# One attention kernel: the key-pair maxima of its first stage, regrouped so that left and right terms have PSUM banks of their own

## What is computed

```
q = layernorm(x) @ W_q + b_q          # 512 x 512: 16 heads of 32
k, v = split(ctx @ W_kv + b_kv)       # 8192 x 512 each
q, k = apply_rope(q, ...), apply_rope(k, ...)
attn = softmax(q @ k.T / sqrt(32))    # per head, 512 x 8192
x = x + (attn @ v) @ W_o + b_o
```

## Time and profile before

| | us |
|---|---|
| median of 3 runs (1836.43 to 1851.83) | 1842.03 |
| profiled execution, its time | 1842.78 |
| profiled execution, span of the profile | 1841.5 |
| PE busy, share of the span | 1653.6 (90%) |
| DVE busy | 1200.4 (65%) |
| ACT busy | 1120.4 (61%) |
| POOL busy | 689.7 (37%) |

### The profile page before, as it was taken

The page is one execution under the profiler, slowest core; times in us unless marked ns, Lnnn a source line. Parts: engine busy times, 40 slices in busy tenths (PEclk is TensorE's granted clock), DMA queues, the critical chain, the costliest instruction groups (busy, mean ns, idle before and its releaser), DMA issues.

```text
span 1841.5 us, 23809 instructions
## 1 busy us (share of the span) xinstructions
PE 1653.6 (90%) x8556; PEld 993.2 (54%) x8556; DVE 1200.4 (65%) x2691; ACT 1120.4 (61%) x1640; POOL 689.7 (37%) x323
## 2 busy tenths in 40 slices
PE   5669899998999965999999999999985998999998
PEld 4535555555555532333333333333574986888886
DVE  5447766777676765999898898898752553222222
ACT  3347666666666754977888888888731654333332
POOL 3166665666657742996000000000050004444442
PEclk7879999999999975999999999999997999999999
DMA  4644455445554437444444444455239003444431
GB/s 151 186 127 127 152 191 160 126 127 162 183 158 126 136 109 182 117 99 108 116 116 115 115 115 117 113 123 119 88 99 251 23 1 107 130 125 127 128 124 57
DMA packets 94949, 231.80 MB, mean 126 GB/s; under 512 B 11324, under 2 KB 11580, under 8 KB 89968
## 3 DMA queue, kind: packets, MB, share of 16 engines
q1 hardware_dynamic: 93792, 227.40, 44.5%
q10 hardware_dynamic: 1040, 2.88, 0.7%
HBM read 150.45 MB, written 59.84 MB: 114 GB/s over the span
## 4 chain that ended last, share of the span: by engine, by line
PE 57%; POOL 14%; DMA 7%; DVE 6%; issue 5%; ACT 5%; SPq 4%; POOLq 0%; ACTq 0%; DVEq 0%
PE PS L621 14%; PE PS L650 12%; PE PS L113 8%; PE PS L114 7%; PE PS L115 7%; DMA cs<-kr 5%; SPq L67 4%; POOL kr L385 4%; POOL kr L382 4%; POOL cs L383 4%; PE PS L418 3%; PE PS L903 2%; DVE rel L429 1%; ACT rel L426 1%; PE PS L660 1%
## 5 line engine op out<-in xcount | busy, mean ns | idle before, releaser
L627 ACT ACTIVATE P<-PS 128x1024 f32<-128x1024 f32 x512 | 494.5, 1024 | 92.5 <-PE PS L621 66.5
L639 DVE TENSOR_TENSOR acc<-acc,P 128x2048 f32<-128x2048 f32 x216 | 507.9, 2416 | 42.3 <-ACT P L627 42.1
L429 DVE CUSTOM_DVE_ANT_0 rel<-PS,rel 128x256 f32<-128x256 f32 x1024 | 373.1, 420 | 182.5 <-ACT rel L426 182.3
L426 ACT ACTIVATE rel<-PS 128x512 f32<-128x512 f32 x512 | 277.9, 596 | 130.0 <-PE PS L418 129.9
L650 PE MATMUL PS<-P,qe 128*32 128x512 f32 x2048 | 273.2, 606 | 0.0
L418 PE MATMUL PS<-khd,qh 32*128 32x512 f32 x1024 | 141.1, 534 | 101.1 <-DVE mpart L429 83.4
L108 POOL TENSOR_TENSOR w3l<-qk,w3h 128x2048 fp32r<-128x2048 f32 x2 | 9.1, 4559 | 490.7 <-ACT w3h L105 490.7
L108 POOL TENSOR_TENSOR El<-We,Eh 128x1536 fp32r<-128x1536 f32 x36 | 126.0, 3501 | 166.3 <-ACT Eh L105 166.2
L418 PEld LDWEIGHTS PS<-khd,qh 32*128 32x128 f32 x1024 | 59.7, 197 | 207.8 <-DVE mpart L429 193.7
L382 POOL TENSOR_TENSOR kr<-kr,cs 128x512 f32<-128x512 f32 x64 | 83.9, 1312 | 209.3 <-DMA cs<-kr 185.1
L1050 DVE TENSOR_TENSOR hf<-sg,PS 128x512 f32<-128x512 f32 x36 | 24.8, 688 | 193.2 <-PE PS L115 190.0
(11 more groups left out here) (208 smaller groups left out, 2876.5 us busy)
## 6 DMA issues: line engine op xcount, KB each, us to landing
khd<-kscr SPq DMA_DIRECT2D x129, 256.0 KB, 4.1
We<-in_w_e SPq DMA_DIRECT2D x36, 768.0 KB, 5.9
y<-in_y SPq DMA_DIRECT2D x16, 1024.0 KB, 7.2
cs<-kr SPq DMA_DIRECT2D x128, 128.0 KB, 6.4
vscr<-cs SPq DMA_DIRECT2D x16, 1024.0 KB, 4.8
kscr<-khd SPq DMA_DIRECT2D x16, 1024.0 KB, 6.8
kscr<-kl SPq DMA_DIRECT2D x16, 1024.0 KB, 7.0
qe<-vscr SPq DMA_DIRECT2D x64, 256.0 KB, 4.7
```

The source lines that it names most:

```text
L426: m = AC.sig(nc.scalar.activation(rel[b][:, :, :], PS[:, 2 * b:2 * b + 2, 256:512], ACT.Relu))
L429: maxfree[b] = DV.sig(nc.vector.tensor_tensor_reduce(out=rel[b][:, j, :], in0=PS[:, 2 * b + j, 0:256], in1=rel[b][:, j, :], scale=1.0, sca ...
L627: expm[s, pr] = spfree[b] = AC.sig(nc.scalar.activation(P[s % 4][:, 2 * pr:2 * pr + 2, :], PS[:, 2 * b:2 * b + 2, :], ACT.Exp, scale=SCALE))
L639: accm[s] = DV.sig(nc.vector.tensor_tensor(a[:, :, :], a[:, :, :], P[s % 4][:, :, :], ALU.add))
```

## The change

`maxima(c, i)` is gone. In its place a step treats two query blocks at once (`qp`, 8 steps for a chunk), in two halves. The three bank pairs are named r0, r1, r2.

1. `maxima_1`: for two query blocks, heads 0 and 1 are multiplied with the key columns themselves into r0, heads 2 and 3 with the difference columns into r1: 8 matmuls of 256 columns. ACT then takes relu of all of r1 (1024 elements).
2. `maxima_2`: heads 2 and 3 with the key columns into r1, heads 0 and 1 with the difference columns into r2: 8 matmuls. It waits for the relu that has just read r1. ACT takes relu of r2 (1024 elements). DVE does its four instructions on r1, then four on r0.

Then the roles turn by one pair (`cycle[0] += 1`). The number of DVE instructions (1024) and of columns streamed is the same; relu instructions are half as many and twice as long; matmuls and weight loads of the maxima are twice as many and half as long.

`mm3` now calls `tick` after each matmul, so a unit has 12 slots, and `at(u, m, fn)` names unit and slot. Places: `y_high` k in unit k of a chunk, slot 4 (before: all four in units 2 and 3); `y_low` unit 3, slot 4; `rope` as before at the end of unit 3; `key_high(c, g)` one unit apart, units 8+g (counted from the start of chunk c), slot 8; `key_low` at the end of unit 11; `maxima_1` and `maxima_2` at slots 2 and 7 of units 9 to 16.

```diff
-        maxfree = [None] * 3
-        pairs = [0]
+        maxfree, cycle, half = [None] * 3, [0], {}
...
+        def score_pairs(c, g, qp, which, left, right):
+            for t in range(2):
+                qt = 2 * qp + t
+                for hd in range(4):
+                    rows = slice(32 * hd, 32 * hd + 32)
+                    keys = slice(256, 512) if hd // 2 == which else slice(512, 768)
+                    o = PS[:, 2 * (left if hd // 2 == which else right) + hd % 2, t * 256:(t + 1) * 256]
+                    ins = nc.tensor.matmul(o, qh[rows, g, qt * 128:(qt + 1) * 128], khd[c % 2][rows, g, keys],
+                                           start=True, stop=True)
+            return PE.sig(ins)
...
+        def maxima_1(c, i):
+            g, qp = i // 2, i % 2
+            r = [(cycle[0] + j) % 3 for j in range(3)]
+            PE.wait(t_qsplit, khm[c, g], khd_m[c, g], maxfree[r[0]], maxfree[r[1]])
+            m = score_pairs(c, g, qp, 0, r[0], r[1])
+            half[c, i] = r, relu(0, r[1], m)
+        def maxima_2(c, i):
+            g, qp = i // 2, i % 2
+            r, t_r = half.pop((c, i))
+            cycle[0] += 1
+            PE.wait(maxfree[r[2]], t_r)
+            max_last[c] = m = score_pairs(c, g, qp, 1, r[1], r[2])
+            maxfree[r[2]] = t_l = relu(1, r[2], m)
+            maxfree[r[1]] = larger(c, g, qp, 1, 0, r[1], m, t_r)
+            maxfree[r[0]] = larger(c, g, qp, 0, 1, r[0], t_l)
...
-                    at_slot(32 * c + 9 + k, y_high, c + 1, k)
-                at_slot(32 * c + 12, y_low, c + 1)
-            at_slot(32 * c + 15, rope, c)
+                    at(8 * c + k, 4, y_high, c + 1, k)
+                at(8 * c + 3, 4, y_low, c + 1)
+            at(8 * c + 3, 11, rope, c)
             for g in range(4):
-                at_slot(32 * c + 38 + g, key_high, c, g)
-            at_slot(32 * c + 41, key_low, c)
-            for i in range(16):
-                at_slot(32 * c + 41 + 2 * i, maxima, c, i)
+                at(8 * c + 8 + g, 8, key_high, c, g)
+            at(8 * c + 11, 11, key_low, c)
+            for i in range(8):
+                at(8 * c + 9 + i, 2, maxima_1, c, i)
+                at(8 * c + 9 + i, 7, maxima_2, c, i)
```

More of the change, by code:

```diff
@@ L112, in mm3 @@
             for k in range(nk):
[L113 to L117, removed]
+                for i, (a_, b_) in enumerate(((lh, rh), (lh, rl), (ll, rh))):
+                    ins = nc.tensor.matmul(o, a_(k), b_(k), start=first and k + i == 0,
+                                           stop=last and k == nk - 1 and i == 2)
+                    if between and k + i < nk + 1:
+                        between()
             return ins
@@ L206, in build @@
         ql = sb1("ql", [128, 4, 512], F32R)
-        rel = [sb1(f"rel{i}", [128, 2, 256]) for i in range(3)]
+        rel = [sb1(f"rel{i}", [128, 2, 2, 256]) for i in range(2)]
         l_q = lane("l_q")
@@ L405, in key_low @@
             kl_out[c] = l_ko.dma(SP, kscr[:, c, 1].rearrange("g p n -> p g n"), kl[:, :, :])
[L407 to L430, removed]
-                        op0=ALU.add, op1=ALU.max, accum_out=mpart[:, 4 * (2 * hp + j) + g, qt, c:c + 1]))
@@ new lines, in relu, with larger @@
+        def relu(i, b, m):
+            AC.wait(m)
+            return AC.sig(nc.scalar.activation(rel[i][:, :, :, :],
+                                               PS[:, 2 * b:2 * b + 2, :].rearrange("p j (t n) -> p j t n", t=2), ACT.Relu))
+        def larger(c, g, qp, hp, i, b, *marks):
+            DV.wait(*marks)
+            for j in range(2):
+                for t in range(2):
+                    m = DV.sig(nc.vector.tensor_tensor_reduce(
+                        out=rel[i][:, j, t, :], in0=PS[:, 2 * b + j, t * 256:(t + 1) * 256], in1=rel[i][:, j, t, :],
+                        scale=1.0, scalar=NEG, op0=ALU.add, op1=ALU.max,
+                        accum_out=mpart[:, 4 * (2 * hp + j) + g, 2 * qp + t, c:c + 1]))
+            return m
@@ L457, in build, with at @@
         AC.wait(t_wks, t_wvs)
+        def at(u, m, fn, *a_):
+            at_slot(12 * u + m, fn, *a_)
         for c in range(NCH):
```

## The result

The changed kernel takes 1875.23 us (median of 4 runs, 1871.59 to 1875.39) against 1844.97 for the kernel before, measured beside it (4 runs, 1836.43 to 1851.83): a ratio of 1.0162 with a 95% interval from 1.0114 to 1.0209. It is slower by 1.6%, and it lies outside the range on record (1820 to 1866). The profiled execution took 1875.11 us, its span is 1873.8.

What follows compares the result with a forecast made beforehand. The kernel was taken as bound by a POOL and DMA ring of 38.15 us per chunk in the first stage; a new ring of 39.3 through PE and ACT put the reduction at 725 against 721.91, hence 1845 us, range 1820 to 1866.

Steps and rivals of the forecast that it cites:

- The ring that closes through PE and ACT: First stage, per chunk: rotated group 0, two units on PE, ACT's last `y_high`, `y_low`, `key_low`, swap; 39.3 us with half clock.
- Swap: Ring's last term, from the end of `key_low` to the next rotation: 12.29 us, taken over from the old order.
- what would prove it wrong: Signs against the forecast: L368 starts with no wait on ACT, or the swap takes clearly other than 12.3 us.
- Sum: First stage: chunk 1 rotates at 134.5, twelve rings of 39.3, chunks 14 and 15, tail; 725 against 721.91, so +3 us.
- Rotation, 1.65, two units, 2.26: Ring terms: group 0's rotation 3.88; difference and start 1.65; two units 8.36; group, relu, last `y_high` and start 2.26 us.
- Clock: Two units behind PE's idle time, on the ring's path: half clock costs 0 to 6.0 us; 1.6 taken.
- PE's idle time: PE needs 33.4 us of a ring, so idles some 3 to 4 us before each chunk's first `maxima_1`.
- Second rounds (third rival): L414 groups on PE: second round's weight loads exposed, 0.2 us per group gives 1858, 0.43 gives 1881; chance 0.17.
- Waits of `maxima_2` on the relu and of the bank pairs: Maxima steps: relu ready after 1.7 us against PE's 1.9; four L429 take 1.46 of 2.3 us; both fit narrowly.
- Port: DVE's difference of group 3 meets `y_low` on POOL and loses 1 to 2 us, covered by PE's slack.
- Chances: Whole kernel: faster by over 1% (below 1824) 0.23, slower (above 1860) 0.23, within 0.54.
- DVE shut out: DVE blocked through `y_low` and `key_low` together, PE idles 5 us more: ring about 41, 1868 us; chance 0.06.

Runs made afterwards that it cites:

- early split: The changed kernel with all four `y_high` and `y_low` in a chunk's first unit, ahead of the `maxima_1` that waits for rotated group 0: 1851.65 us.
- groups only: The kernel before with the new `maxima_1` and `maxima_2`, every function in its old slot: 1839.79 us, ratio 0.9992.
- swap first: The changed kernel with the swap issued right behind its four projections, ahead of `key_low`, both writes to `kscr` and the load of `y`: 1802.74 us.

## Why the prediction was wrong

*The mechanism: right.* The ring that closes through PE and ACT is there. L368 stands behind a wait for ACT in every chunk (48.0 us in 15 waits, 22.2 of them in the first), and cutting that path (early split) takes 0.9 us off the ring ahead of the swap, and another 1.0 off the swap. Keeping the clock on that path takes 1.3 off ahead of the swap. Beside the kernel before, the way from the rotation to the swap has grown by 1.15 us, and that is also what the forecast gave for the whole ring (39.3 for 38.15).

*Swap: the step that failed.* The sum had "12.29 to the next rotation", with the remark that the swap "now stands behind a write of 1 MB instead of a load of 1 MB". It looked at the one transfer directly ahead. But the same move had brought the load of `y` and the write of `khd`, formerly 8 us earlier, to within 5 us of the swap, as the order printed with the change shows. The term measures 13.95: over twelve rings that is 20 us of the 25.7 missed, and in chunks 14 and 15 it is another 1.7 and 1.1 (idle 12.09 and 11.49 where 10.4 was taken). Taking one of the three from ahead of the swap brings swap to rotation from 13.5 back to 11.3 or 11.7 (two experiments, two different megabytes); with all three behind it, it is 9.6. The prediction named this as what would prove it wrong; it should have been a rival with a price. A bound could have been read from the trace of before: by my estimate, three transfers of 1.05 MB at the 426 GB/s that its DMA view shows at best are 7.4 us, of which only about 5 would have passed before the swap; before, 8.2 had.
Why the three transfers make SP's issuing longer stays open. It is not their number: before, three in 8.2 us go with 5.84 us, while `khd` or `y` behind the swap leave only two and still have 7.25. All seven kernels with 6.8 to 7.5 us have the write of `kl` handed over directly ahead of the swap (0.4 to 0.5 us), the kernel before and groups only (5.84 and 5.88) have the load of `y` there; no experiment separates this from the rest. That it alone makes the loss is excluded: with `kl` in its place the two experiments have swap to rotation at 11.3 and 11.7.

The Trainium skill (DMA: Bandwidth & Descriptors, Queues, rings and completion order) says that on each DMA engine the descriptors of one queue are consumed in ring order; by that, what is handed over ahead of the swap on the same queue delays it even if nobody waits for it. The runs here agree as to the landing: with the write of `khd` gone from ahead of the swap, the pieces land 1.3 us sooner after their issue.

*Sum, redone with the measured terms.* Chunk 1 rotates at 135.79 for 134.5. Twelve rings at (628.38 - 135.79) / 12 = 41.05 instead of 39.3 give 21 us. Chunk 14 comes after 39.27 instead of 37.4 (idle before it 12.09 where 10.4 was taken), chunk 15 after 36.41 instead of 33.9. From there to the reduction 46.6 us pass for a forecast of 47.6. So 1.3 + 21 + 1.9 + 2.5 - 1.0 = 25.7 us, and 725 + 25.7 = 750.7 is the measured 750.64: these five terms carry the whole miss.

*Rotation, 1.65, two units, 2.26:* right to a tenth of a microsecond each.

*Clock:* 1.6 taken, 1.74 read in one ring (1.4 to 2.4 in the others), and 1.26 of a ring gained where the clock was kept. The 1.6 was taken over from the old kernel, whose idle times were others; that it fits is luck.

*PE's idle time* was to be 3 to 4 us and is 5.97. The two misses behind it: the ring is longer, and a unit takes 4.06 us where 4.18 was taken, so that eight of them and the clock's 1.74 make only 34.2 of the 40.2.

*Second rounds (third rival):* fell. A group of eight matmuls of 256 columns takes 0.51 us at full clock, as the four of 512 did (0.50 and 0.51). From its start to the next projection's it is 0.45 us for 0.43, so the second round's loads are exposed by 0.02 at most. The rule of the Trainium skill that was set against this change (TensorE: Matmul & The Clock Gate, Part 3) does not show up in these rows; the same section also lets a load into the background weight buffer go ahead, and that fits them.

*Waits of `maxima_2` on the relu and of the bank pairs:* right, they fit; PE's waits for `mpart` in the first stage (60 to 700 us) fell from 70.8 us to 7.8 in the view by line. The gain lay off the path: the waits for the difference of a rotated group, L394, took its place (13.7 us before, 102.6 after).

*Port:* 1 to 2 us a chunk were forecast for DVE's difference beside `y_low`. L394 takes 1.260 us on average for 1.013 before (both from 60 to 680 us), four in a chunk: 1.0 us, covered by PE's slack. In the ring above the difference of group 3 starts at 321.58, 2.9 us into L368, and takes 2.03 us, to just behind L368's end at 323.33. The Trainium skill's rule (SBUF — State Buffer, Who interferes with whom), by which the later one waits, agrees with this row.

*Chances:* slower by over 1% had 0.23, and a ring of 41 stood in the text only under two rivals that did not happen (the 41 of the second, DVE shut out, is not worked out from its 5 us). The range was too narrow at the top because its unknown costs were those of PE and ACT, and none was a DMA's.

## What to carry to other kernels

When a change moves a piece of work past another on a queue, list for before and after every transfer handed over in the ten microseconds ahead of the one on the path, with its size: one that nobody waits for still delays what follows it on the same queue. A transfer whose inputs are ready early belongs ahead of those whose inputs come late, since in an in-order queue it inherits their waits; here that was worth more (72 us from the changed kernel) than the changed kernel had lost. Small periodic pieces of work on an engine between two others are to be moved with care even when they look free: gathering four casts and `y_low` in one unit gave 24 us in one kernel and took 41 in another.

## What was not expected of the hardware

- Issuing the same eight DMAs of 128 KB takes SP 5.1 to 5.9 us with nothing large handed over in the 7 us ahead (swap first, chunks 1 to 15), 5.6 to 6.2 with the load of `y` directly ahead (before, chunks 1 to 13), and 7.0 to 8.1 in the changed kernel (chunks 1 to 13), with the write of `kl` directly ahead.
- From the first issue of the swap to the rotation it is 9.6 us with all three megabytes behind it, 10.7 to 12.0 with two ahead or with three spread over 8 us, 12.5 with three in 6 us (early split), and 13.4 to 13.9 with three in 5 us.
- Twenty matmuls of no use in PE's idle time raise the granted clock of 134 to 400 us from 0.91 to 0.98 and make the kernel 18.8 us faster than without them.
